# Packed lane and tile words, one-hots shared between two engines, and a router that picks on shifted logits

## What is computed

```python
logits = xf @ gate_w.T
probs = jax.nn.softmax(logits, axis=-1)
vals, idx = jax.lax.top_k(probs, K)                 # K = 2 of E = 8
w = vals / (vals.sum(-1, keepdims=True) + 1e-08)    # first layer; the second layer uses vals as they are
...
out = jnp.einsum('ned,ne->nd', eo, comb)            # weighted sum of the chosen experts' outputs
```

## Time and profile before

| what | value |
|---|---|
| three runs | 1193.18, 1194.84 and 1196.61 us, median 1194.84 us |
| profiled execution | 1198.09 us, its span 1196.3 us |
| mean granted TensorE clock | 0.861 of full |
| busy share of the span | PE 75%, DVE 64%, ACT 51%, POOL 43% |

### The profile page before, as it was taken

How to read it: one execution, slowest core, us unless ns; L and a number is a source line. 1 busy time by engine, 2 the same in 40 slices (tenths; PEclk the granted TensorE clock), 3 DMA queues, 4 the chain that set the end, 5 groups by cost and what they waited for, 6 DMA issues and landing times.

```text
span 1196.3 us, 25602 instructions
## 1 busy us (share of the span) xinstructions
PE 892.9 (75%) x7009; PEld 723.3 (60%) x7009; DVE 765.6 (64%) x1916; ACT 613.6 (51%) x1345; POOL 508.7 (43%) x408
## 2 busy tenths in 40 slices
PE   5320286855589999999994751579999999999975
PEld 4200165741367777777773640168888888888863
DVE  5899788999455555655653788835555555555540
ACT  4447286857365565565662245835434444444433
POOL 1288000000256666666663230045556555555540
PEclk8655598975699999999997875579999999999996
DMA  8249274990378888888887533255666465664438
GB/s 256 71 141 316 70 252 153 295 295 1 80 185 207 200 203 207 205 202 211 202 204 216 190 115 102 79 111 118 126 117 141 76 144 114 120 136 75 75 62 281
DMA packets 208566, 190.01 MB, mean 159 GB/s; under 512 B 98752, under 2 KB 184200, under 8 KB 208392
## 3 DMA queue, kind: packets, MB, share of 16 engines
q1 hardware_dynamic: 148344, 108.48, 32.2%
q0 software_dynamic: 27440, 38.97, 18.9%
q10 hardware_dynamic: 32736, 42.02, 11.4%
HBM read 111.22 MB, written 58.79 MB: 142 GB/s over the span
## 4 chain that ended last, share of the span: by engine, by line
PE 36%; DVE 19%; issue 15%; DMA 14%; ACTq 7%; ACT 7%; SPq 1%; DVEq 1%; POOL 0%; POOLq 0%
PE bank L796 15%; PE bank L774 13%; DMA wreg<-in_L_ffn_w_dram 5%; DMA rows_y<-region 4%; PE bank L838 2%; ACTq L313 2%; DVE region L1194 2%; DVE xt L1215 2%; ACT region L1065 2%; ACTq L1033 2%; ACT region L1069 2%; DVE region L1192 1%; PE bank L682 1%; DVE region L1583 1%; ACTq L314 1%
## 5 line engine op out<-in xcount | busy, mean ns | idle before, releaser
L774 PE MATMUL bank<-xt,wreg 128*128 x3360 | 385.1, 275 | 28.4 <-DMA xt<-region 25.7
L774 PEld LDWEIGHTS bank<-xt,wreg 128*128 128x128 f16 x3360 | 327.8, 99 | 79.9 <-issue 38.2
L542 POOL DMA_INDIRECT rows_y<-region x140 | 249.3, 1781 | 179.8 <-ACT region L1091 92.4
L796 PE MATMUL bank<-wreg,region 128*128 128x256 f16 x2520 | 294.5, 273 | 22.9 <-ACT region L1069 16.6
L796 PEld LDWEIGHTS bank<-wreg,region 128*128 128x128 f16 x2520 | 234.6, 98 | 77.5 <-ACT region L1069 30.6
L492 POOL DMA_INDIRECT region<-rows_x,region x148 | 151.6, 1024 | 270.6 <-DVE region L1492 153.5
L1074 ACT ACTIVATE region<-bank,b_t,wreg 128x256 f32<-128x256 f32 x280 | 136.0, 560 | 21.2 <-PE bank L774 20.2
L1091 ACT ACTIVATE region<-region 128x256 f32<-128x256 f32 x70 | 31.7, 500 | 193.6 <-DVE region L1598 183.0
L1065 ACT ACTIVATE region<-bank,fac 128x256 f32<-128x256 f32 x140 | 58.3, 465 | 97.7 <-PE bank L774 55.2
L1593 DVE SCALAR_TENSOR_TENSOR region<-region,wreg 128x512 f16<-128x512 f32 x140 | 105.1, 751 | 5.0
L1590 DVE TENSOR_SCALAR region<-region,wreg 128x512 f16<-128x512 f32 x140 | 70.0, 500 | 51.8 <-ACT region L1074 51.7
(11 more groups left out here) (273 smaller groups left out, 1120.3 us busy)
## 6 DMA issues: line engine op xcount, KB each, us to landing
wreg<-in_L_ffn_w_dram SPq DMA_DIRECT2D x80, 512.0 KB, 5.9
wreg<-in_L_ffn_w_dram ACTq DMA_DIRECT2D x72, 256.0 KB
split_v<-wreg ACTq DMA_DIRECT2D x36, 512.0 KB
wreg<-split_v SPq DMA_DIRECT2D x32, 512.0 KB
rows_x<-region SPq DMA_DIRECT2D x16, 512.0 KB, 5.1
rows_y<-tok SPq DMA_DIRECT2D x16, 512.0 KB, 6.1
tok<-rows_y SPq DMA_DIRECT2D x16, 512.0 KB, 6.0
wreg<-in_x_dram SPq DMA_DIRECT2D x4, 1024.0 KB, 9.5
```

What stands on the lines that cost most here:

```text
L542: nc.gpsimd.indirect_dma_start(rows_y[f], bass.IndirectOffsetOnAxis(ap=now[:, b, g_, 1:2], axis=0), y_rows[:, g_, :], None, compute_op=ALU ...
L774: last = pe.matmul(to, block, x_cols[:, bass.ds(b, 1), :, xs_, k, :].rearrange("p j r n -> p (j r) n"), start=(k == 0 and ws_ + xs_ == 0), ...
L796: last = pe.matmul(yb[:, r * C:(r + 1) * C], lhs[:, c, r * P:(r + 1) * P], block, start=first, stop=end, skip_group_check=True)
```

## The change

1. **One word for lane and tile.** GpSimd makes a constant `pair_word` at the start: 64 words of 32 bits on each partition, the low half the lane number and the high half the tile number, both in half precision. `hot_pair` is the one-hot of groups times that word, 80 words of 32 bits, in one vector instruction for each entry; read as half precision it is the 160-column moving operand, with lane and tile columns interleaved. It takes the place of L1466, L1468, L1020 and L1021, and of L1455 and L1456.
2. **Three of eight lane one-hots on ScalarE.** For entries 2, 4 and 7 of a pass, ScalarE makes `hot_lane` in two steps: the square of (lane - column), then relu(1 - that). The vector engine makes the other five.
3. **Picking on shifted logits.** The two experts are picked on the logits less their largest; the exponential of all and a second, small exponential of the two picked values run on ScalarE meanwhile. Sum, reciprocal and weights follow after the one-hots have gone to TensorE.
4. Four more constant instructions on GpSimd, and `CONSTS` goes from 18 to 22.

```diff
@@ constants, GpSimd
+            ids_i = scratch[:, 3 * P:3 * P + 2 * NT].bitcast(I32)
+            nc.gpsimd.iota(ids_i, [[1, 2 * NT]], base=1, channel_multiplier=0).then_inc(consts, 1)
+            nc.gpsimd.memset(lane[:, 3:4], 1.0).then_inc(consts, 1)
+            nc.gpsimd.tensor_copy(pair_halves[:, :, 0], int_e[:, 1, 0:1].to_broadcast([P, 2 * NT])).then_inc(consts, 1)
+            nc.gpsimd.tensor_copy(pair_halves[:, :, 1], ids_i).then_inc(consts, 1)
@@ lists, TensorE
-                        pe.wait_ge(ids_listed, 8 * HB * f + 8 * i + b + 1)
-                        pe.matmul(yb[:, 0:2 * GROUPS], hot_lane[:, b], hot_group[:, b].rearrange("p v n -> p (v n)"),
+                        pe.wait_ge(listed, 8 * HB * f + 8 * i + b + 1)
+                        if b in BY_ACT:
+                            pe.wait_ge(lanes_listed, 3 * HB * f + 3 * i + BY_ACT.index(b) + 1)
+                        pe.matmul(yb[:, 0:2 * GROUPS], hot_lane[:, b], hot_pair[:, b].bitcast(F16),
@@ ScalarE
+                act.wait_ge(exp_in, 2 * f + 2)
+                act.activation(tok_w.rearrange("p t k -> p k t"), top[:, 0:2, :], ACT.Exp).then_inc(exp_out, 1)
...
-                with act.Fori(0, HB) as i:
-                    for b in range(8):
-                        act.wait_ge(listed, 8 * HB * f + 8 * i + b + 1)
-                        if b % 2 == 0:
-                            act.activation(hot_group[:, b, 0], hot_one[:, b], ACT.Copy, scale=lane[:, 0:1])
-                        act.activation(hot_group[:, b, 1], hot_one[:, b], ACT.Copy,
-                                       scale=id_f[:, b % 2, bass.ds(4 * i + b // 2, 1)]).then_inc(ids_listed, 1)
+                def lanes(i):
+                    for n, b in enumerate(BY_ACT):
+                        if f or not isinstance(i, int):
+                            act.wait_ge(lanes_listed, 3 * HB * f + 3 * i + n - 2)
+                        act.activation(far_sq[:, n], count16[:], ACT.Square, scale=-1.0,
+                                       bias=lane_f[:, b % 2, bass.ds(4 * i + b // 2, 1)]).then_inc(far_known, 1)
+                    for n, b in enumerate(BY_ACT):
+                        if f or not isinstance(i, int):
+                            act.wait_ge(list_taken, 8 * HB * f + 8 * i + b - 7)
+                        act.wait_ge(far_known, 3 * HB * f + 3 * i + n + 1)
+                        act.activation(hot_lane[:, b], far_sq[:, n], ACT.Relu, scale=-1.0, bias=lane[:, 3:4]).then_inc(lanes_listed, 1)
+                act.wait_ge(slots_known, f + 1)
+                pairs(act, lanes)
@@ picking, VectorE
-                chain(dve.tensor_reduce(red[:, 0, :], ex, AX.X, ALU.add))
-                chain(dve.reciprocal(red[:, 1, :], red[:, 0, :]))
-                chain(dve.tensor_tensor(ex, ex, over_e(red[:, 1, :]), ALU.mult))
-                for k, hot in enumerate((hot1, hot2)):
-                    chain(dve.tensor_reduce(top[:, k, :], ex, AX.X, ALU.max))
-                    ...
+                chain(dve.scalar_tensor_tensor(eq, lg, 0.0, over_t(rank[:]), ALU.is_equal, ALU.mult))
+                chain(dve.tensor_reduce(red[:, 0, :], eq, AX.X, ALU.max))
+                chain(dve.tensor_tensor(hot1, eq, over_e(red[:, 0, :]), ALU.is_equal))
+                chain(dve.scalar_tensor_tensor(slot_f, hot1, -1e30, lg, ALU.mult, ALU.add))
+                chain(dve.memset(top[:, 0, :], 0.0))
+                dve.tensor_reduce(top[:, 1, :], slot_f, AX.X, ALU.max).then_inc(exp_in, 1)
+                dve.wait_ge(exp_in, 2 * f + 2)
+                chain(dve.tensor_tensor(eq, slot_f, over_e(top[:, 1, :]), ALU.is_equal))
+                chain(dve.tensor_tensor(eq, eq, over_t(rank[:]), ALU.mult))
+                chain(dve.tensor_reduce(red[:, 0, :], eq, AX.X, ALU.max))
+                chain(dve.tensor_tensor(hot2, eq, over_e(red[:, 0, :]), ALU.is_equal))
+                dve.tensor_tensor(hots16[:], hot1, hot2, ALU.add).then_inc(hots_ready, 1)
+                dve.wait_ge(exp_out, 2 * f + 2)
+                chain(dve.tensor_reduce(red[:, 0, :], ex, AX.X, ALU.add))
+                chain(dve.reciprocal(red[:, 1, :], red[:, 0, :]))
                 if f == 0:
+                    chain(dve.tensor_tensor(vals, vals, by_k(red[:, 1, :]), ALU.mult))
+                    chain(dve.tensor_tensor(red[:, 0, :], vals[:, 0], vals[:, 1], ALU.add))
                     chain(dve.tensor_scalar(red[:, 0, :], red[:, 0, :], 1e-8, None, ALU.add))
                     chain(dve.reciprocal(red[:, 1, :], red[:, 0, :]))
+                dve.tensor_tensor(vals, vals, by_k(red[:, 1, :]), ALU.mult).then_inc(weights_kept[f], 1)
@@ lists, VectorE
-                chain(dve.memset(flat(red), 1.0))
-                chain(dve.tensor_tensor_scan(flat(id_f), flat(red), flat(red), 0.0, ALU.mult, ALU.add))
...
-                        dve.tensor_scalar(hot_lane[:, b], count16[:], at(lane_f), None, ALU.is_equal)
-                        if b % 2:
-                            dve.tensor_scalar(hot_group[:, b, 0], count16[:, 0:GROUPS], at(group_f), lane[:, 0:1],
-                                              ALU.is_equal, ALU.mult)
-                        dve.tensor_scalar(hot_one[:, b], count16[:, 0:GROUPS], at(group_f), None, ALU.is_equal).then_inc(listed, 1)
+                        if b not in BY_ACT:
+                            dve.tensor_scalar(hot_lane[:, b], count16[:], at(lane_f), None, ALU.is_equal)
+                        dve.tensor_scalar(hot_pair[:, b], count16[:, 0:GROUPS], at(group_f), pair_word[:, bass.ds(k * NT + 4 * i + q, 1)],
+                                          ALU.is_equal, ALU.mult).then_inc(listed, 1)
```

More of the change, by code:

```diff
@@ L178, in bass_metaformer @@
         lane_f, group_f = (by_choice(xn_all[:, 512 + 64 * q:576 + 64 * q]) for q in range(2))
-        id_f = by_choice(xt_all[:, 960:1024])
-        hot_group = xt_all[:, 0:8 * GROUPS].bitcast(F16).rearrange("p (b v n) -> p b v n", v=2, n=GROUPS)
-        hot_one = xt_all[:, 8 * GROUPS:12 * GROUPS].bitcast(F16).rearrange("p (b n) -> p b n", n=GROUPS)
+        hot_pair = xt_all[:, 0:8 * GROUPS].rearrange("p (b n) -> p b n", n=GROUPS)
+        far_sq = xt_all[:, 8 * GROUPS:8 * GROUPS + 3 * P // 2].bitcast(F16).rearrange("p (b n) -> p b n", n=P)
+        BY_ACT = (2, 4, 7)
         pad_f, sum_f, to_f = (xn_all[:, 704 + GROUPS * q:704 + GROUPS * (q + 1)] for q in range(3))
@@ L202, in bass_metaformer @@
         count16 = sb("count16", [P, P], F16)
-        lane = sb("lane", [P, 3])
+        lane = sb("lane", [P, 4])
+        pair_word = wreg[:, 32704:32704 + 2 * NT]
+        pair_halves = pair_word.bitcast(F16).rearrange("p (s v) -> p s v", v=2)
         b1_t = sb("b1_t", [P, E, 8])
@@ L268, in bass_metaformer @@
         rows_hi, rows_ready = sem2("rows_hi"), sem2("rows_ready")
[L269 to L270 removed]
+        logits_kept, exp_in, exp_out = sem2("logits_kept"), sem("exp_in"), sem("exp_out")
+        hots_ready, counts_psum, moves_ready, rows_stored = sem("hots_ready"), sem("counts_psum"), two("moves_ready"), two("rows_stored")
         listed, list_taken = sem("listed"), sem("list_taken")
+        slots_known, far_known, lanes_listed = sem("slots_known"), sem("far_known"), sem("lanes_listed")
         lists_copied = two("lists_copied")
[L273 removed]
         tok_loaded = [[sem(f"tok_loaded_{n}") for n in range(4)], x_loaded]
@@ L438, in _ @@
             load_tokens(1)
-        CONSTS = 18
+        CONSTS = 22
         @block.gpsimd
@@ L728, in routing @@
                 pe.matmul(misc[:, 0:NT * E], before16, flat_hots, start=True, stop=True)
-                pe.matmul(misc[:, NT * E:2 * NT * E], ones16[:, 0:1].to_broadcast([P, P]), flat_hots, start=True, stop=True).then_inc(counts_psum[f], 1)
+                pe.matmul(misc[:, NT * E:2 * NT * E], ones16[:, 0:1].to_broadcast([P, P]), flat_hots, start=True, stop=True).then_inc(counts_psum, 1)
                 def lists(i, start=False, stop=False):
                     for b in range(8):
-                        pe.wait_ge(ids_listed, 8 * HB * f + 8 * i + b + 1)
-                        pe.matmul(yb[:, 0:2 * GROUPS], hot_lane[:, b], hot_group[:, b].rearrange("p v n -> p (v n)"),
+                        pe.wait_ge(listed, 8 * HB * f + 8 * i + b + 1)
+                        if b in BY_ACT:
+                            pe.wait_ge(lanes_listed, 3 * HB * f + 3 * i + BY_ACT.index(b) + 1)
+                        pe.matmul(yb[:, 0:2 * GROUPS], hot_lane[:, b], hot_pair[:, b].bitcast(F16),
                                   start=start and b == 0, stop=stop and b == 7).then_inc(list_taken, 1)
@@ L1409, in route @@
-                dve.tensor_tensor(hots16[:], hot1, hot2, ALU.add).then_inc(hots_ready[f], 1)
+                by_k = lambda v: v.unsqueeze(1).to_broadcast([P, 2, NT])
+                vals = tok_w.rearrange("p t k -> p k t")
                 if f == 0:
-                    chain(dve.tensor_tensor(red[:, 0, :], top[:, 0, :], top[:, 1, :], ALU.add))
```

(8 more changed lines are left out.)

20 lines of the change are left out of this document (11 added, 9 removed).

## The result

| | before | after |
|---|---|---|
| median of the runs, us | 1195.72 (1193.18 to 1199.14, 4 runs) | 1177.67 (1174.80 to 1179.49, 4 runs) |
| profiled execution / its span, us | 1198.09 / 1196.3 | 1174.8 / 1173.1 |
| mean granted TensorE clock | 0.861 | 0.868 |

The ratio is 0.985, with a 95% interval of 0.982 to 0.9875: 18 us faster. A second set of runs of the same changed kernel, on another chip, gave 0.987 (0.9835 to 0.991), which is 15 us. The two profiled executions lie 23 us apart, since the one of after is the lowest of its runs and the one of before near the top of its own. What can be read to 0.02 us is the routing stretch, which repeats to that in two executions of the changed kernel.

The account below looks back on a forecast made before the run. The vector engine's chain to the first fetch was taken to bound both routing stretches. Lists 5.5 us a layer plus head 1.8 and 2.7 made 15.5 us, from 1194.84 to 1179.3 us; range 1174.5 to 1188.

Parts of the forecast that it names:

- Rival D: Wait for the first fetch: a store or fetch ends it instead, so the gain doesn't arrive, about 1194 us; chance 0.04.
- Head: Routing steps from the largest logit's subtraction to the lists: 1.8 us less in layer 0, 2.7 in layer 1.
- `hot_pair`: New one-hot instruction in the lists: 0.235 us between starts, eight a pass, in a pass of 2.67 us.
- Rival A: Lists: `hot_pair` runs in the slow form, 0.275 us spacing; 11.1 us less in all, 1183.7 us; chance 0.11.
- E: Lists: `hot_pair` costs no more than L1466 and the sequencer keeps up; 1175.3 us, chance counted within the forecast's 0.66.
- the middle value: Lists: `hot_pair` at 0.235 us spacing, its 32-bit output charged 24 ns more than L1466, between bounds 0.21 and 0.275.
- ScalarE: Lists: six activations a pass at 0.30 us each, 1.8 us, under the vector engine's 2.67, with 0.87 to spare.
- rival C: Lists: a table load for square or relu in every pass, 17 us lost against 4.5 gained, 1207 us; chance 0.04.
- The sequencer: Looped list passes: 1.03 us of address operations a pass against 0.91, just enough; 0.3 us a layer given back.
- rival B: Looped list passes: sequencer bounds them, 21 address operations instead of 16; 7.5 us less in all, 1187.3 us; chance 0.15.
- a pass of over 3 us: Lists: a pass taking this long, where 2.67 us was forecast, would show the prediction wrong.
- gaps put down to issue: Vector engine in the lists: idle gaps the profile attributes to issue would point to the sequencer as the bound.

Follow-up runs that it names:

- four_unrolled: Changed kernel with the vector engine's eight list passes written out and a fourth lane one-hot of each pass on ScalarE; 1176.06 us, ratio 0.9825 to the kernel before.
- all_vector: Changed kernel, still looped, with all eight lane one-hots on the vector engine and none on ScalarE; 1188.3 us, ratio 0.9939 to the kernel before.
- old_unrolled: Kernel before the change with only the vector engine's eight list passes written out; 1192.87 us, ratio 0.9988 to the kernel before.
- after_again: The changed kernel once more, unchanged, with more rounds, against the kernel before; 1187.26 us, ratio 0.9872.
- held: Changed kernel with 20 chained idle multiplications on the vector engine ahead of the lists in each layer; ratio 1.0024 to the kernel before.
- unrolled: Changed kernel with the vector engine's eight list passes written out, ScalarE and TensorE still looped; 1184.29 us, ratio 0.9845 to the kernel before.

## Why the prediction was right, and where its sum was off

**The path.** That the vector engine's way to its last routing step sets the end of both stretches held. In all nine rows of the table below the first the measured change follows the routing stretch, from -20.9 beside -19.3 to +2.9 beside +3.3, never more than 2 us apart but for the first set of after, where it is 4.8. Rival D (a store or fetch ends the wait) is out: the first fetch was released by L1509, with a route 16.8 us longer than after's the end moved along, and with one 5.8 us shorter it moved the right way, though there the intervals overlap.

**Head.** The ten steps took 4.73 where 4.71 stood in the sum. The three steps behind the one-hots cost 1.03 in layer 0 (1.15 forecast) and 0.19 in layer 1 (0.25 forecast); dropping L1455 and L1456 gave 0.51 (0.47 forecast). In all 1.97 and 2.82 us, forecast as 1.8 and 2.7.

**`hot_pair`.** 317 ns and 0.231 between starts, taken as 319 and 0.235. Rival A (0.275) and E (0.21) are out: half precision in and 32 bits out is no slow form. The Trainium skill (VectorE: DVE Perf Modes, What auto-detection actually checks) gives two elements a cycle to a one-source operation in SBUF whatever the type. The rows agree in size: `hot_pair` takes 21 ns more than L1466's 296 for the same 80 elements, against the 24 of the middle value and the 64 or so of rival A.

**ScalarE.** Taken at 0.30 an activation, 0.292 by the trace of four_unrolled, where they follow each other without a gap. No load of a table came with squares and relus, so rival C is out. The Trainium skill (ScalarE: Activation LUTs, Rules for kernel authors) sends relu to the vector engine. Per one-hot the rows agree (0.163 against two steps of 0.292). For this kernel, all_vector shows that following it costs 3.25 us a layer, because the two engines run side by side and the vector engine is the longer one. The prediction had the pass 0.47 longer by that rule; where no pass is late it is 0.49 (3.15 against 2.66).

**The sequencer: the term that was too small.** The prediction counted 1.03 us of address operations a pass against 0.91, called it "just enough" and gave back 0.3 us a layer. It leaned on a lead of 1.7 to 1.8 us "from first to last", but these are the first value of layer 0 and the last of layer 1. Within layer 0 the lead fell, and the sequencer's pass of 3.39 us could be read before the change (see old_unrolled). The durations were nearly right (93 ns for `hot_pair`, one operation and not the two of rival B; 65 instead of 57 for the lane), but they are not all the sequencer does. A late pass of 3.0 to 3.2 us holds 13 instructions with 1.07 us of such operations. The profile lists some of the rest, six or seven further operations of 40 ns (L1480) and the loop's own three (L243, which another loop has too):

```profile
L1480 DVEq ALU_OP  x91: 40/40/40, 273.4 to 749.9; - x91
L243 DVEq ALU_OP  x21: 40/40/40, 28.1 to 750.2; - x21
L243 DVEq COMPARE_BRANCH  x21: 50/56/63, 28.2 to 750.3; - x21
L243 DVEq FUSED_REGOPS  x14: 63/63/77, 272.5 to 747.4; - x14
```

Much of a late pass's loss stands at the loop's turn. From the start of the last instruction of one pass to the start of the first of the next are 0.58 us in layer 0, where it is 0.23 in the early passes: 0.35 of the 0.54 lost in a pass of 3.20. The prediction took no price for any of this from a row. The term cost 2.17 us in layer 0 and 0.97 in layer 1. Rival B was right about the engine and the place and wrong about its cause and size: not 21 operations, and not from the first looped pass on, but once the lead was used up, after three passes in layer 0 and five in layer 1. (Its own sum is off too: the written-out pass and the tail that it names gain 0.7 + 0.4 = 1.1 us a layer and not 1.5.)

**A sign that came.** The prediction named a pass of over 3 us as a sign that it is wrong, and six of the 14 stretches between passes took 3.02 to 3.20. What failed with it is the statement that the sequencer keeps up, and not the path: eight passes with their tail still got 3.78 and 4.96 us shorter. Its sign for rival B, gaps put down to issue, did not come, since the profile put them down to TensorE. Whoever looks for that sign alone misses it.

**The sum.** Without the sequencer's loss the lists fell by 27.75 - 21.80 = 5.95 us, where 5.8 was forecast. With it they fell by 3.78 and 4.96, where 5.5 was. Together with the head and 0.01 us of difference in the last steps, 5.75 + 7.78 = 13.5 us of routing, where 15.5 was forecast. The measured gain is 18.3 us in one set of runs and 15.4 in the other. The forecast of 1179.3 lies near the median of 1177.67 partly by luck: an over-estimate of 2 us stands against a surplus of up to 5, which no row explains. It was 1.9 in after_again, and the expert stage's own scatter is larger than it.

**What stays open.** The prediction named a change in the length of the stretch behind the first fetch as a sign against it. That stretch varies by 10 us in one and the same kernel, so the runs can't tell. Why a late pass takes 3.20 us in layer 0, 3.07 in layer 1 and 3.0 in layer 0 of held was not found either. The traces show the places, the loop's turn above all, and not the reason; and since unrolled takes out addresses, computed wait values and branch together, no run prices them one by one.

## What to carry to other kernels

When a looped pass gets shorter on an engine, count again what its sequencer has to do in the pass, all of it and not the address operations alone, and look at how far ahead of its instruction each pass's address is computed, pass by pass and stretch by stretch: a lead that shrinks, if only by 0.04 us a pass, is the warning. Writing a short loop out took the cost away here. The releaser that a profile names is the semaphore of the wait, not always its reason; take the other candidate away and see if the gap stays. And where the rest of the kernel scatters by more than the effect, compare the stretch that repeats, and hold the medians of several versions against it.

## What the runs showed of the hardware that was not expected

- A looped pass of 13 vector instructions, each with an address or two computed at run time, could not be handed on in less than 3.0 to 3.2 us, where the instructions themselves take 2.66; written out, all passes take 2.65 or 2.66. In the pass of 16 instructions of all_vector late passes take 3.5 to 3.6 us against 3.16. The kernel before, with 20 instructions and 16 address operations in 3.35 us, lost nothing, but in layer 0 its sequencer already took about 3.39 a pass.
- The cost comes late: the sequencer's lead, 1.7 us at the second pass, hides it for three to six passes, so a mean over the passes, or a look at the first, shows a smaller price than the last passes pay.
- The turn of one and the same loop on the vector engine's sequencer, from its branch to its next operation, took 0.29 us in layer 0 and 0.19 in layer 1, in the kernel before and in the changed one, and 0.19 in both layers of held.
- One and the same kernel's layer-0 expert stage took 310.6 us in one execution and 320.8 in another, with a routing stretch equal to 0.02 us in both.
